# Two context attentions on one core: all probability tiles summed by GpSimd, and the queue order around them

## What is computed

```
def latent_xattn(latents, context):          # layer 1, 16 heads of 64
    q = layer_norm(latents) @ Wq
    k, v = split(layer_norm(context) @ Wkv)
    k = apply_rope(k, cos, sin)
    p = exp(clip(q k^T / 8, -11, 11)); p = p / sum(p)
    return (p @ v) @ Wo + bo
def cross_xattn(query, ctx):                 # layer 3, 16 heads of 64
    q, k, v = query @ Wq + bq, ctx @ Wk + bk, ctx @ Wv + bv
    return (softmax(q k^T / 8) @ v) @ Wo + bo
x = x + latent_xattn(layernorm(x), ctx)
x = x + routed_experts(layernorm(x))
x = x + cross_xattn(layernorm(x), ctx)
x = x + gated_self_attention(x)
```

## Time and profile before

| | |
|---|---|
| median of 3 runs | 3098.83 us (3094.63 to 3098.9) |
| profiled execution | 3097.14 us; span of its instructions 3095.3 us |
| granted TensorE clock, mean | 0.898 |
| latent layer, first to last sum | 74.9 to 936.7 us |
| cross layer, first to last sum | 1213.3 to 2269.4 us |
| rest | expert layer between them, self attention behind |
| PE / DVE / ACT / POOL busy | 80% / 68% / 36% / 35% of the span |
| additions of probabilities on DVE | 96 latent (288.3 us busy), 64 cross (92.1 us) |
| additions of probabilities on POOL | 96 latent (266.3 us), 128 cross (303.7 us) |

### The profile page before, as it was taken

The page is one execution under the profiler, slowest core; times in us unless marked ns, Lnnn a source line. Parts: engine busy times, 40 slices in busy tenths (PEclk is TensorE's granted clock), DMA queues, the critical chain, the costliest instruction groups (busy, mean ns, idle before and its releaser), DMA issues. The chain is left out here.

```text
span 3095.3 us, 35966 instructions
## 1 busy us (share of the span) xinstructions
PE 2470.9 (80%) x12832; PEld 1507.2 (49%) x12832; DVE 2094.8 (68%) x3274; ACT 1116.1 (36%) x1554; POOL 1082.3 (35%) x731
## 2 busy tenths in 40 slices
PE   5999999999995979999998999998955546455464
PEld 4555556556554756555555655555533223233232
DVE  6997997987884865555555455545526867768675
ACT  4444444454451014434334334434413213222131
POOL 4543443443440014222322223222331523525235
PEclk9999999999997989999999999999976768676686
DMA  3001001000001130000000000000010001000000
GB/s 97 11 1 35 1 1 35 1 1 14 1 1 55 41 102 23 1 1 21 15 1 21 14 1 1 1 14 1 1 32 13 14 0 34 0 21 14 0 21 7
DMA packets 70788, 51.66 MB, mean 17 GB/s; under 512 B 12706, under 2 KB 70626, under 8 KB 70626
## 3 DMA queue, kind: packets, MB, share of 16 engines
q1 hardware_dynamic: 70628, 49.55, 5.3%
HBM read 41.15 MB, written 8.39 MB: 16 GB/s over the span
## 5 line engine op out<-in xcount | busy, mean ns | idle before, releaser
L1644 DVE TENSOR_REDUCE cross_part<-cross_ring 128x1 f32<-128x512 f32 x512 | 321.1, 682 | 76.6 <-PE cross_ring L1781 75.9
L1527 ACT ACTIVATE cross_probs<-cross_scores 128x1024 f32<-128x1024 f32 x256 | 251.0, 1024 | 241.4 <-PE cross_scores L1813 240.8
L1448 POOL TENSOR_TENSOR cross_acc_pool<-cross_acc_pool,cross_probs 128x1024 f32<-128x1024 f32 x96 | 228.0, 2375 | 253.0 <-ACT cross_probs L1527 248.2
L1527 ACT ACTIVATE latent_probs<-latent_scores 128x1024 f32<-128x1024 f32 x256 | 248.7, 1020 | 90.2 <-PE latent_scores L1809 76.0
L1617 DVE SCALAR_TENSOR_TENSOR cross_KL<-cross_ring,cross_bqkv,cross_KH 128x512 fp32r<-128x512 f32 x64 | 47.9, 750 | 306.2 <-ACT cross_KH L1499 306.2
L1781 PE MATMUL cross_ring<-cross_KH,cross_QH 64*128 64x512 f32 x512 | 176.6, 481 | 94.6 <-DVE cross_newt L1680 49.7
L1829 PE MATMUL cross_outT<-cross_probs,cross_VN 128*64 128x512 f32 x1024 | 250.8, 611 | 0.0
L1829 PE MATMUL latent_outT<-latent_probs,latent_VN 128*64 128x512 f32 x1024 | 248.2, 605 | 1.4 <-DVE latent_probs L1659 1.4
L1448 POOL TENSOR_TENSOR cross_acc_pool<-cross_probs 128x1024 f32<-128x1024 f32 x32 | 75.7, 2365 | 437.4 <-PE cross_ring L1781 242.6
L1448 POOL TENSOR_TENSOR latent_acc_pool<-latent_acc_pool,latent_probs 128x1024 f32<-128x1024 f32 x64 | 177.5, 2774 | 114.8 <-DVE latent_probs L1659 114.8
L1659 DVE TENSOR_SCALAR latent_probs<-latent_probs 128x1024 f32<-128x1024 f32 x256 | 200.1, 818 | 17.9 <-ACT latent_probs L1527 17.7
(11 more groups left out here) (304 smaller groups left out, 6230.8 us busy)
## 6 DMA issues: line engine op xcount, KB each, us to landing
latent_C<-in_ctx_dram SPq DMA_DIRECT2D x4, 1024.0 KB, 6.2
cross_C<-in_ctx_dram SPq DMA_DIRECT2D x4, 1024.0 KB, 7.9
latent_XN<-in_x_dram SPq DMA_DIRECT2D x4, 512.0 KB, 3.6
latent_WRAW<-in_L_xattn_Wkv_dram SPq DMA_DIRECT2D x16, 128.0 KB, 2.4
latent_X<-in_x_dram SPq DMA_DIRECT2D x4, 512.0 KB, 3.6
x_after<-latent_X SPq DMA_DIRECT2D x4, 512.0 KB, 2.9
experts_raw<-in_L_ffn_expert_w_dram SPq DMA_DIRECT2D x1, 2048.0 KB
experts_XN<-x_after SPq DMA_DIRECT2D x4, 512.0 KB, 3.8
```

What stands on the lines that cost most here:

```text
L1448: nc.gpsimd.tensor_tensor(acc_pool[:, :, :], first[:, :, :], probs[g % PROBS][:, :, :], ALU.add)\
L1527: nc.scalar.activation(probs[g % PROBS][:, :, :], scores[g % 2][:, :, :], ACT.Exp, scale=SCALE)\
L1644: nc.vector.reduce_max(part[:, qt, h, i:i + 1], bank[:, :], AX.X).then_inc(taken, 1)
```

## The change

`BY_POOL` becomes all eight tiles in both layers, so POOL makes seven additions per step, VectorE none, and `sum` has two products instead of four. In the latent layer the last `kv` unit of a step moves from the last part of the step before into part 0 of the step itself, each of the others one place later or alone in its part, and the two `kT` items move from `tail` behind the values to `mid`, between scores and values, of part 1 (second half of the keys) and part 3 (first half for the next step). In the list, `tail` now stands ahead of the additions. In the cross layer the 16 maxima, which came in groups of three and two (three and three in part 3), come in pairs: before the two `S`, between them (a new list `between`), and behind them, in parts 1 and 2, and in two pairs in part 3. `guess` may stand up to two ring items behind its `sum`, but never behind `norm`.

```diff
-    front, mid, tail, late = ([[] for _ in range(steps * parts)] for _ in range(4))
+    front, between, mid, tail, late = ([[] for _ in range(steps * parts)] for _ in range(5))
...
+        if latent:
+            put(tail, s, 0, ("kv", s, 3))
+            put(mid, s, 1, ("kT", s, 1))
         if s > 0 and latent:
-            put(tail, s, 0, ("kT", s, 1), ("sum", s - 1))
+            put(tail, s, 0, ("sum", s - 1))
             put(late, s, 0, ("norm", s - 1))
-        elif latent:
-            put(tail, s, 0, ("kT", s, 1))
...
-                tail[s * parts] = [("kT", s, 1), turn(n, "c", 0), ("sum", s - 1), turn(n, "c", 1)]
-                put(tail, s, 1, turn(n, "x", 0), ("kv", s + 1, 0), turn(n, "x", 1), ("kv", s + 1, 1))
-                put(tail, s, 2, turn(n, "c", 0, 1), ("q", s + 1), turn(n, "c", 1, 1), ("kT", s + 1, 0))
-                put(tail, s, 3, ("kv", s + 1, 2), ("kv", s + 1, 3))
+                tail[s * parts] = [("kv", s, 3), turn(n, "c", 0), ("sum", s - 1), turn(n, "c", 1)]
+                put(tail, s, 1, turn(n, "x", 0), ("kv", s + 1, 0), turn(n, "x", 1))
+                put(tail, s, 2, turn(n, "c", 0, 1), ("kv", s + 1, 1), turn(n, "c", 1, 1), ("q", s + 1))
             elif more:
-                put(tail, s, 1, ("kv", s + 1, 0), ("kv", s + 1, 1))
-                put(tail, s, 2, ("q", s + 1), ("kT", s + 1, 0))
-                put(tail, s, 3, ("kv", s + 1, 2), ("kv", s + 1, 3))
+                put(tail, s, 1, ("kv", s + 1, 0))
+                put(tail, s, 2, ("kv", s + 1, 1), ("q", s + 1))
+            if more:
+                put(mid, s, 3, ("kT", s + 1, 0))
+                put(tail, s, 3, ("kv", s + 1, 2))
...
-            for d, (n, m) in enumerate(((3, 2), (3, 2), (3, 3))):
-                put(front, s, d + 1, *maxima[:n])
-                put(mid, s, d + 1, *maxima[n:n + m])
-                maxima = maxima[n + m:]
+            for d, places in enumerate(((front, between, mid), (front, between, mid), (front, between))):
+                for place in places:
+                    put(place, s, d + 1, *maxima[:2])
+                    maxima = maxima[2:]
...
-        plan += [("q", 0)] + [("kv", 0, t) for t in range(2)] + [("kT", 0, 0), ("kv", 0, 2), ("kv", 0, 3)]
+        plan += [("q", 0)] + [("kv", 0, t) for t in range(2)] + [("kT", 0, 0), ("kv", 0, 2)]
...
-        scores = [("S", s, 2 * d), ("S", s, 2 * d + 1)]
+        scores = [("S", s, 2 * d), *between[n], ("S", s, 2 * d + 1)]
...
-        plan += clips + adds + tail[n] + late[n]
+        plan += clips + tail[n] + adds + late[n]
...
-        while plan[behind][0] not in RING and plan[behind][0] != "norm":
+        units = 0
+        while plan[behind][0] != "norm" and units < BANKS - 1:
+            units += plan[behind][0] in RING
             behind += 1
-        plan.insert(behind + (plan[behind][0] in RING), ("guess", item[1]))
+        plan.insert(behind, ("guess", item[1]))
...
-    BY_POOL = (0, 2, 4, 6) if latent else (0, 2, 4, 5, 6)
+    BY_POOL = tuple(range(KT))
     BY_DVE = tuple(t for t in range(KT) if t not in BY_POOL)
+    POOL_ADDS, DVE_ADDS = (max(len(tiles) - 1, 0) for tiles in (BY_POOL, BY_DVE))
...
-                    pe.wait_ge(dve_added, (s + 1) * (len(BY_DVE) - 1))
-                    pe.wait_ge(pool_added, (s + 1) * (len(BY_POOL) - 1))
-                    for i, acc in enumerate((acc_dve, acc_pool)):
+                    if BY_DVE:
+                        pe.wait_ge(dve_added, (s + 1) * DVE_ADDS)
+                    if BY_POOL:
+                        pe.wait_ge(pool_added, (s + 1) * POOL_ADDS)
+                    accs = [acc_dve] * bool(BY_DVE) + [acc_pool] * bool(BY_POOL)
+                    for acc in accs:
```

More of the change, by code:

```diff
@@ L1445, in _ @@
                     else:
-                        pool.wait_ge(pool_added, s * (len(BY_POOL) - 1) + j - 1)
+                        pool.wait_ge(pool_added, s * POOL_ADDS + j - 1)
                         first = acc_pool
@@ L1524, in _ @@
                         was, at = divmod(g - PROBS, KT)
-                        mine, added = (BY_POOL, pool_added) if at in BY_POOL else (BY_DVE, dve_added)
-                        act.wait_ge(added, was * (len(mine) - 1) + adds_until(at, mine))
+                        if at in BY_POOL:
+                            act.wait_ge(pool_added, was * POOL_ADDS + adds_until(at, BY_POOL))
+                        else:
+                            act.wait_ge(dve_added, was * DVE_ADDS + adds_until(at, BY_DVE))
                     nc.scalar.activation(probs[g % PROBS][:, :, :], scores[g % 2][:, :, :], ACT.Exp, scale=SCALE)\
@@ L1670, in _ @@
                     else:
-                        dve.wait_ge(dve_added, s * (len(BY_DVE) - 1) + j - 1)
+                        dve.wait_ge(dve_added, s * DVE_ADDS + j - 1)
                         first = acc_dve
@@ L1833, in _ @@
                     s = item[1]
-                    pe.wait_ge(dve_added, (s + 1) * (len(BY_DVE) - 1))
-                    pe.wait_ge(pool_added, (s + 1) * (len(BY_POOL) - 1))
-                    for i, acc in enumerate((acc_dve, acc_pool)):
+                    if BY_DVE:
[4 more added lines that the diff above has]
+                    for acc in accs:
                         for h in range(2):
-                            last = nc.tensor.matmul(bank[HEAD[h], :], ones[:, :], acc[:, h, :], start=i == 0, stop=i == 1)
+                            last = nc.tensor.matmul(bank[HEAD[h], :], ones[:, :], acc[:, h, :], start=acc is accs[0],
+                                                    stop=acc is accs[-1])
                     last.then_inc(full, 1)
```

## The result

The changed kernel takes **3255.6 us** (median of three, 3253.7 to 3255.8) against 3098.83: a ratio of 1.0506, 95% interval 1.0485 to 1.0527. It is slower by 157 us, where 84 were forecast, and 34 us above the range's upper end. Its profiled execution has a span of 3253.8 us (3095.3 before).

A forecast was written before the change was run, and what follows sets the result against it. VectorE's queue was taken to set the latent pace, TensorE close behind; in the cross layer TensorE's timeline, with VectorE only where it frees banks. 3097.1 + 44 latent + 40 cross = 3181, adjusted to 3182 us; range 3092 to 3222.

The forecast's parts named there:

- 28.0 and 26.0: Latent plain step in us: 28.0 as forecast, 26.0 if neither clips nor their queue cost anything; 25.65 before.
- rival (a): Both layers: faster, as relieving VectorE decides and POOL's work fits beside it; 3070 or 3018 us; chance 0.17.
- Latent size: Latent layer: +44 us in all, from ordinary steps +41, opening steps -3, entering steps +4 and ends +2.
- The walk: Latent layer: one plain step followed engine by engine from the end of `sum`, giving 28.0 us against 25.65.
- The head of line: Latent layer, POOL's queue: `KR` stands in front of its part's additions, which wait for `kv`, copy and rotation.
- Cross size: Cross layer: +1.3 us a step from +3.0, +0.05, -0.8 and -0.91, times 31, so +40 us.
- `L1689` standing behind addition 2: Cross layer: this VectorE instruction waits for POOL's second addition until 5.3 us; `AV` comes 3.0 us later.
- the prediction's own sign of being wrong: Cross layer: the forecast would be wrong if `L1689` were still at 0.69 us instead of near 2.8.
- the forecast's meeting: Cross layer, each step: a `norm` instruction on VectorE stands behind a POOL addition, delaying the reduction and fourth maximum.
- rival (b): Cross layer: `L1689` slips in ahead of addition 2, -21 us there, only the latent chain costs; 3122 us; chance 0.13.
- Costed at nothing: Cross layer: POOL's seven additions cost nothing, covered by TensorE's step with 7 us to spare.
- the latent bound: Latent layer: -8 us if clips and their queue cost nothing, +60 if each meeting costs 0.5 us more.

The follow-up runs named there:

- e5: Changed kernel with 6 unread filler products on TensorE ahead of its wait for POOL's last addition in latent steps: 3216.6 us, ratio 1.0376.
- e7: Changed kernel with the latent clip cut to 32 of a tile's 1024 columns: 3162.5 us, ratio 1.0193.
- e9: e5 with latent normalizing instructions from the second batch on replaced by batch statistics and the Newton ones by memsets, rows unnormalized: 3197.6 us, ratio 1.0313.
- e4: Changed kernel with the additions put ahead of `tail` in the list again: 3267.8 us, ratio 1.0558.
- e2: Changed kernel with the old split of additions between POOL and VectorE, only the new order kept: 3262.8 us, ratio 1.0536.
- e11: Kernel before with all cross additions on POOL and `q` ahead of `K`, without POOL's wait for `norm`: 3097.7 us, ratio 0.9990.
- e3: Kernel before with all additions on POOL and the old order in both layers: 3152.1 us, ratio 1.0175.
- e8: Kernel before with all cross additions on POOL, `q` ahead of `K`, and each step's first addition held behind `norm`: 3072.9 us, ratio 0.9918.
- e10: Changed kernel with the next step's `q` ahead of its second `K` unit in the cross layer: 3273.6 us, ratio 1.0552.

## Why the prediction was right or wrong

**Direction and mechanism: right.** It said slower because seven additions and four `KR` in order, with their meetings, end behind TensorE's work, so that `sum` waits for POOL some 4 us a step. Measured: 95.2 us in 28 waits, 3.4 each, 3.66 in the plain step. POOL's idle time before `KR0` is 6.29 us against the 4.5 forecast, longer only by what the slow clock puts on TensorE (4.54 in e5). That the clips are the difference between 28.0 and 26.0 is shown by e7 (26.0; their meetings and their own time together), the 28.0 by e5 (28.1). That rival (a) is wrong is shown by both layers.

**Latent size: wrong, +44 against +125.7.** The miss of 82 us has two steps.
- *A term left out, 44 us.* The walk took TensorE's durations at the full clock of the earlier trace rows, although it made TensorE wait 4 us in every step. The granted clock was 0.5 from `sum` on, and `sum`, two `S` and `kT` took 2.7 us more. It was in the prediction's own reach: the step before had no such wait, and its 1.00 could not be carried to one that has. In the cross layer of the kernel before, 13 steps have 3.4 us of half clock, starting some 3 us behind the logarithm, after a wait of about 1.65 us. 44 is the least that the clock cost: e5 still has 25 us of half clock more than the kernel before, which at half speed would be up to 12 us of the next term, as an estimate.
- *A term mis-sized, 37 us.* For the 24 ordinary steps the working was 24 x 28.0 = 672, plus 7 for roots and splits: 679. With the clock restored (e5) they take 708, with the normalization's meetings gone too (e9) 693. So 15.5 of these 29 us are small VectorE instructions that stand behind additions, which the prediction hadn't priced at all (with the clock that the longer waits cost, 10 us less of it at half in e9): it set clips and rotations against POOL's additions, and read the one plain step of the earlier trace rows, which has no normalization. The other 14 are in the difference between the ordinary and the plain step that existed before (26.57 against 25.65 on average, 22 us in all), of which I had let 7 stand. By e9's trace most of them are the first steps of the batches, where `X` + bias (2.83 us) or, in the first batch, weight splits stand in POOL's queue; the walk had no term for the former. That was read from the trace and not tried by a run. Entering steps cost +8.3 and not +4 (e5), opening ones gained 1.6 (e5) and not 3, the last interval cost 4.0 and not 2.

**The head of line, partly wrong.** The list's new order was called the reason why POOL doesn't fit. e4 puts the additions ahead again and is no faster. The load of POOL with its meetings is what doesn't fit; order decides only where TensorE stands.

**Cross size: near (+29.5 for +40), by luck.** The step that failed is `L1689` standing behind addition 2 in every step. `L1696` is at 0.69 us in 27 of its 32 records, which is the prediction's own sign of being wrong. It takes 2.71 in the 3 steps behind a batch change (35.8 to 37.6 us), but behind `X` + bias and not behind addition 2. e2 has the forecast's meeting in nearly every step, with another addition. In 3 other steps of the changed kernel the first `norm` instruction is blocked instead (2.16 us, about 38). The rest has rival (b)'s order, and at the full clock its -0.7 a step came true: 31.9 us against 32.7 before, although 0.6 of the 0.91 us taken from `sum` comes back as the wait for `q` (18.1 us in 30 waits) and the fourth maximum waits 1.88. But only three plain steps are at the full clock throughout. The half clock rose from 44 to 124 us, and a plain step with 3.4 us of it is 33.5: at 1.6 us for each 3.4 that would be some 38 us, an estimate. With the six blocked steps and the longer last interval (20.2 for 16.8) this turned rival (b)'s -21 into +29.5. The prediction gave this order 0.13 and wrote that it hung on 0.3 us; it hung on 0.05.

**"Costed at nothing"**: seven cross additions on POOL. As to the length of POOL's chain that was right: its last addition ends 7.5 us ahead of the next logarithm (median in e11), where 7 to spare were forecast. As to the layer it was not: e3 has them together with the shorter `sum` at -1.3 us, where the shorter `sum` alone was to bring -28. Keeping them off `norm` (e8 against e11) is worth 21 of the difference.

**The range** took half a microsecond more per meeting as its upper end. It had no case in which TensorE's own speed depends on the wait. Its terms don't quite add up either: 16 for the latent bound and 31 x 0.5 for the cross steps lead from 3182 to 3213 and not to 3222. And the latent bound at steps of 26.0 is, counted as the +44 was, 624 + 7 - 638 + 3 = -4 and not -8. Neither would have changed the outcome.

What stays open: how much of the 2.1 us between e5's and e7's plain steps is meetings and how much is the clips' own time, and why the cross layer has 124 to 150 us at half clock in the changed kernel and in those of its variants with the same cross layer. There the half clock starts 3 to 6 us behind the logarithm, behind waits of 0.60 and 1.88 us; but three steps of the same order stay at the full clock.

## What to carry to other kernels

A wait of some 4 us put into a loop of TensorE must be priced with the slower products behind it; here they added 2.7 us to each plain step, and three pairs of filler products gave it back. POOL and VectorE can be balanced by busy time only if the instructions that block each other don't meet (here additions, clips, `norm` and the small ones of a normalization; not the batch statistics): list every one of them that could stand behind a long POOL instruction, the tiny ones first, and every other POOL instruction that the additions push aside, as `X` + bias here. Then hold POOL back for a moment where VectorE has a short chain on the path (3.5 us of slack a step for 21 us of layer). An outcome that depends on which of two engines is first by less than 0.1 us should be made certain with a wait, not forecast.

## What the runs showed of the hardware

- TensorE's granted clock was 0.5 (1.2 GHz) behind waits of 3.66 us in a busy loop and came back within the next 4 us; with 2.8 us of extra products ahead of the wait and 0.88 us of waiting left (e5), it stayed at 1.00 for the whole step.
- A VectorE multiplication on 128x4 took 2.3 us beside POOL's additions and 0.16 without; batch statistics on 128x256 stayed at 0.41 in both. The Trainium skill (SBUF — State Buffer, § SBUF: two separate sides) says that of two such instructions the one that starts first has the shared ports for its whole length and the other fully blocks; the trace agrees with 2.88 us for an instruction of 0.69 that started 0.01 us behind an addition of 2.34 (e10).
- Two filler products of 512 columns took 0.9 us, not the half that I had expected; the rows had it, as the `sum`'s two products take 0.95.
